# Graph layers: GpSimd also writes one spare column with each row gather

## The reference

```python
s_u = x @ W_u.T + b_u
s_v = x @ W_v.T
e = s_u[src] + s_v[dst]
e = jnp.where(e >= 0, e, 0.2 * e)
m = jax.ops.segment_max(e, dst, num_segments=n_nodes)
e_exp = jnp.exp(e - m[dst])
denom = jax.ops.segment_sum(e_exp, dst, num_segments=n_nodes)
probs = e_exp / denom[dst]
xh = x.reshape(n_nodes, head_dim, num_heads)
msg = xh[src] * probs[:, None, :]
out = jax.ops.segment_sum(msg, dst, num_segments=n_nodes)
```

## Time and profile before

| what | value |
|---|---|
| three timed runs | 5178.16, 5181.27, 5187.05 us (median 5181.27) |
| the profiled execution | span 5191.0 us; the page gives no other time for it |
| busy, share of the span | PE 64%, PEld 46%, DVE 46%, ACT 24%, POOL 44% |
| row gathers on GpSimd | 1856, together 1756.2 us |
| first graph layer | from 509.70 to about 2180 us |
| second graph layer | from 2609.5 to about 4177 us |

### The profile page before, as it was taken

The page is one execution under the profiler, slowest core; times in us unless marked ns, Lnnn a source line. Parts: engine busy times, 40 slices in busy tenths (PEclk is TensorE's granted clock), DMA queues, the critical chain, the costliest instruction groups (busy, mean ns, idle before and its releaser), DMA issues. The chain is left out here.

```text
span 5191.0 us, 77476 instructions
## 1 busy us (share of the span) xinstructions
PE 3340.9 (64%) x13712; PEld 2365.6 (46%) x13713; DVE 2395.9 (46%) x5335; ACT 1269.3 (24%) x5289; POOL 2284.2 (44%) x2343
## 2 busy tenths in 40 slices
PE   4600666667677677698945445545555547999998
PEld 3400333344444444365823333333333335989897
DVE  4500566666666666686434444444444436111111
ACT  2200233333333333342300000000000034333333
POOL 5160455555555555400355555555555540333333
PEclk9855788888888888898967777777777757999999
DMA  8441233323333333200133333333333342666665
GB/s 200 131 126 30 75 76 77 79 76 79 79 78 80 81 81 81 71 0 2 53 77 84 83 82 85 82 82 87 84 84 85 86 125 95 172 170 171 171 171 135
DMA packets 298775, 489.06 MB, mean 94 GB/s; under 512 B 151906, under 2 KB 199984, under 8 KB 298216
## 3 DMA queue, kind: packets, MB, share of 16 engines
q0 software_dynamic: 127312, 325.41, 25.5%
q1 hardware_dynamic: 159535, 159.18, 10.5%
q10 hardware_dynamic: 11872, 3.84, 0.3%
HBM read 430.09 MB, written 58.63 MB: 94 GB/s over the span
## 5 line engine op out<-in xcount | busy, mean ns | idle before, releaser
L865 POOL DMA_INDIRECT g_rows<-rows,g_recs x1856 | 1756.2, 946 | 1624.1 <-DVE g_msg L1019 905.9
L903 PE MATMUL g_pA<-g_msg,k_ident 128*128 128x264 f32 x3712 | 1091.1, 445 | 154.1 <-DVE g_msg L1019 96.1
L903 PEld LDWEIGHTS g_pA<-g_msg,k_ident 128*128 128x128 f32 x3712 | 787.4, 223 | 498.2 <-issue 360.1
L905 PE MATMUL g_pA<-g_accs,k_ident 128*128 128x264 f32 x928 | 368.7, 485 | 840.8 <-DVE g_accs L1026 565.9
L894 PE MATMUL g_pE<-g_ew,g_recT 128*128 128x512 f32 x936 | 581.6, 754 | 296.9 <-ACT g_recT L934 170.8
L1019 DVE TENSOR_TENSOR g_msg<-g_rows,g_pp 128x1024 f32 (+1 forms) x464 | 564.9, 1217 | 293.5 <-ACT g_pp L959 233.8
L905 PEld LDWEIGHTS g_pA<-g_accs,k_ident 128*128 128x128 f32 x928 | 186.5, 224 | 952.3 <-DVE g_accs L1026 624.2
L954 ACT ACTIVATE g_msg<-g_dd (+1 forms) x464 | 113.5, 245 | 1788.0 <-DVE g_dd L1065 1194.5
L894 PEld LDWEIGHTS g_pE<-g_ew,g_recT 128*128 128x128 f32 x936 | 198.9, 230 | 531.2 <-issue 466.1
L1965 PE MATMUL e_pY<-e_w,e_hT 128*128 x1632 | 375.0, 383 | 23.3 <-issue 22.6
L1954 PEld LDWEIGHTS e_pH<-e_xT,e_w 128*128 128x128 f32 x3264 | 382.3, 193 | 5.2
(11 more groups left out here) (410 smaller groups left out, 3580.7 us busy)
## 6 DMA issues: line engine op xcount, KB each, us to landing
e_w<-in_L_ffn_W SPq DMA_DIRECT2D x110, 1024.0 KB
g_rows<-rows,g_recs POOLq DMA_INDIRECT x1856
g_recs<-slots SPq DMA_DIRECT2D x468, 8.0 KB
tok<-e_xall SPq DMA_DIRECT2D x7, 910.0 KB
rows<-p_row SPq DMA_DIRECT2D x50, 119.0 KB
own<-p_row SPq DMA_DIRECT2D x50, 119.0 KB
p_x<-in_x SPq DMA_DIRECT2D x1, 5600.0 KB
own<-p_x SPq DMA_DIRECT2D x1, 5600.0 KB
```

What stands on the lines that cost most here:

```text
L865: pool.indirect_dma_start(out=rows[:, r, j, :], out_offset=None, in_=rows_d, in_offset=bass.IndirectOffsetOnAxis(ap=recs[:, r, 4 * j:4 * j ...
L903: t_.matmul(pA[:, b, 0:MW], K["ident"][:], msg[:, b, j, :], start=(j == 0), stop=False)
L905: t_.matmul(pA[:, b, 0:MW], K["ident"][:], accs[:], start=False, stop=True).then_inc(agg_ok, 1)
```

## The change

A new tile `beat` holds one number per partition. Behind every row gather of both graph layers GpSimd now writes a zero into it, with a memset that raises the new counter `beaten`. Behind each gather but the first of a layer, and ahead of its memset, GpSimd waits until the memset before has raised `beaten`, and raises `pace`. Nobody else reads `beat` or `beaten`.

```diff
@@ -771,6 +771,7 @@
         den = m.sb(L + "den", [Q, H])
+        beat = m.sb(L + "beat", [Q, 1])
         if not vscale:
...
@@ -865,6 +866,10 @@
                             pool.indirect_dma_start(out=rows[:, r, j, :], out_offset=None, in_=rows_d,
                                                     in_offset=bass.IndirectOffsetOnAxis(ap=recs[:, r, 4 * j:4 * j + 1].bitcast(I32), axis=0)
                                                     ).then_inc(rows_in[r], 16)
+                            if not (first and r == 0 and j == 0):
+                                pool.wait_ge(beaten, 4 * C * u + C * r + j)
+                                pool.sem_inc(pace, 1)
+                            pool.memset(beat[:], 0.0).then_inc(beaten, 1)
                 gather(0, True)
                 with pool.Fori(1, n2 + 2) as u:
                     gather(u, False)
```

More of the change, by code:

```diff
@@ L793, in graph @@
         recT_ps = S("recT_ps"); recT_ok = S("recT_ok"); enc_ok = S("enc_ok"); enc_free = S("enc_free"); lane_ok = S("lane_ok")
-        dd_ok = S("dd_ok"); pp_ok = S("pp_ok"); cs_ok = S("cs_ok"); msg_ok = S("msg_ok"); acc_ok = S("acc_ok"); agg_ok = S("agg_ok"); x_ok = S("x_ok")
+        dd_ok = S("dd_ok"); pp_ok = S("pp_ok"); beaten = S("beaten"); cs_ok = S("cs_ok"); msg_ok = S("msg_ok"); acc_ok = S("acc_ok"); agg_ok = S("agg_ok"); x_ok = S("x_ok")
         row_of = lambda ap: ap.rearrange("p a h -> p (a h)")
```

## The result

The changed kernel takes 5212.8 us (median of four runs, 5206.98 to 5218.3), the kernel before 5184.16 us beside it: a ratio of 1.0059, 95% interval 1.0044 to 1.0073. The forecast was 4870 us. The profiled execution's span is 5204.9 us.

A forecast was written before the change was run, and what follows sets the result against it. Bound: a mutual one in both layers, where held engines free no buffers, GpSimd stops, and the overhang drains. GpSimd's 223 us hidden, the wait 0, 315 given back: 5191 - 315 = 4876, said as 4870 us; range 4700 to 5080.

The forecast's parts named there:

- The overhang: Behind each gather something takes 1.43 us while gathers come each 1.25, so 0.18 us piles up per gather in a burst.
- the holds: Stretches in both graph layers when SyncE, VectorE and ScalarE were said to be held until what piles up behind gathers drains.
- The pitch: Time from one gather's start to the next on GpSimd: from 1.25 to 1.37 us, with ends of 1.21 and 1.51.
- The term of 223 us: GpSimd's added time over all gathers, 1856 x 0.12 us, taken to lie under its 905.9 us of standing.
- the relief of 315 us: Half of ScalarE's 284.7 and VectorE's 346.2 us of waits without a named releaser, to be given back in the graph layers.
- hidden: Rival: GpSimd's added work fits into its 905.9 us of standing and the holds stay; time stays at 5181 us; chance 0.14.
- The wait: GpSimd's wait for the memset of one gather earlier, covered by a gather of 0.95 us, so counted as 0.
- Serial: Rival: GpSimd's wait isn't covered, each gather takes 2.00 us, layers 1856 us each, time 5654 us; chance 0.09.
- Stretched holds: Rival: others are held while GpSimd's queue is busy, bursts grow 0.12 us per gather, 5404 us; chance 0.22 with the port.
- The port: Related price: memsets lock the port VectorE and GpSimd share, 0.09 us each, up to +167 us; in stretched holds' 0.22.
- Full relief by self-throttling: Rival: held-back memset completions slow GpSimd to 1.45 us per gather, nothing piles up, layers 1346 us each, 4634 us; chance 0.17.

The follow-up runs named there:

- steps3: Kernel before plus three already fulfilled waits, each with a raise of `pace`, behind each gather in both layers, no memset: 5092.6 us, ratio 0.9850.
- before_again: The kernel before, unchanged, run and profiled once more: 5172.6 us, with 5174.7 beside it.
- l0_steps: Kernel before plus one already fulfilled wait with a raise of `pace` behind each gather, first layer only, no memset: 5137.4 us, ratio 1.0068.

## Why the prediction was wrong

**The overhang: right.** "1.43 us behind each gather, a new one each 1.25" is what the runs bear out from both sides: at 1.25 the holds are there, at 1.44 they are fewer (most of all in the first layer), at 1.52 to 1.54 gone in the second layer and few in the first, and the engines return 1.43 us per gather after the change too. The Trainium skill (Perfetto Trace Analysis, "DMA Instruction — SWDGE (GPSIMD)") says that the profile ends such an instruction when its descriptors are written, and that the DMA engines go on moving data behind that end. The trace agrees: by the DMA packets in the first layer of before, where the recorded gather is 0.95 us long, the first packet of rows starts 1.64 us after the gather's start and the last signal of their landing comes at 2.46 (medians). But these transfers are not what piles up: the twelfth gather of a burst has the same 1.64 and 2.48 us as the first (1.63 and 2.44), so the rows keep up with a gather each 1.25 us while the queue steps fall behind. What it is that holds the other queues, no run showed.

**The pitch: wrong, and this is the step that failed.** The prediction put x, the time from a gather's end to its memset, at 0.16 us from a row of another instruction, and the pitch at 1.37. Measured: x is 0, the memset 0.11, and 0.19 follow; the sum is 1.25. The term of 223 us is 0, and with it goes the relief of 315 us that was to follow from the wider pitch. The low end of the range for x was there (1.21), and the text even said what it means: the memset falls into the gap. But a gap of 0.30 behind every gather, with nothing waiting for anything, is the first place that a small instruction of the same engine goes to; it should have been the value taken. With an unchanged pitch the same sum says no relief, 5181 us. That is the time of the rival "hidden", given 0.14, though it had another reason (holds that the pitch doesn't touch); and the loss of 29 us is outside its 10 us, so no branch of the prediction has the result for its own reason.

**The relief per microsecond: too good as well.** At 1.37 us the text let most holds vanish, 315 us. No run has an even pitch of 1.37. But at 1.44, above the 1.42, only 177 us came back (0.9654), and it took 1.52 to give 330 (0.9363). The spacing has to leave room.

**The wait: half right.** It costs no pitch. What the text didn't see is that it puts two queue steps per gather on GpSimd, which can be held like anyone's. "GpSimd's own waits never took over 17 ns" was read as if GpSimd were exempt; in before its queue had few steps, three to four per chunk.

**The rivals.** Serial (2.00 us per gather): no. Stretched holds: no, the bursts are not longer per gather and the return still follows their number. The port: VectorE's busy time is 2395.9 us before and 2397.0 after, 1.1 us more where this rival had up to 167, so the memsets held it for next to nothing; the rule of the Trainium skill that the prediction cited (SBUF — State Buffer, "SBUF: two separate sides") allows that for a memset, which reads nothing. Full relief by self-throttling: not in the change; steps3 shows something of it (1.36 and 1.43 us inside a chunk, 0.985 of the time), and the time that the text gave it (4634 us) left out that a layer at 1.45 us keeps holds. The busy time of the engines, before and after:

```profile
PE 3340.9 (64%) x13712; PEld 2365.6 (46%) x13713; DVE 2395.9 (46%) x5335; ACT 1269.3 (24%) x5289; POOL 2284.2 (44%) x2343
PE 3379.6 (65%) x13712; PEld 2391.1 (46%) x13713; DVE 2397.0 (46%) x5335; ACT 1267.7 (24%) x5289; POOL 2493.8 (48%) x4199
```

**The 0.6%.** Shown: it is the first layer's (0.79%, against -0.32% in the second), and in that layer a queue step and a memset behind each gather each cost something of their own (0.68 and 0.38%). Argued, not shown: that the loss comes through the holds. For it: the step costs nothing in the version with next to none, and the held time moved the way of the layers (457 to 528 us in the first, 453 to 412 in the second). Against it: held time is a rough measure, since the second layer has 379 to 481 us of it in every version whose gathers follow each other at under 1.5 us without pauses, while its length goes from 1415 to 1567. Open: by which way an added step or memset lengthens the holds of the others, while the pitch and the 1.43 us stay, and why the parts don't add in both layers. The layers' lengths have to do with how the chunks fall into bursts (in before's first layer a chunk takes 7.2 us in bursts of eight gathers and 7.5 in bursts of twelve, medians), but the number of such bursts doesn't decide: with bursts ended by a pause of over 2.0 us from start to start, before has 26 of twelve, before_again 30 and after 37; with 2.4 us it is 39, 41 and 39.

## What to carry to other kernels

Where an engine stands in a short gap behind each of many equal instructions, price a small added instruction at nothing first, and look for what it does to the queue and not to the engine. Where waits without a named releaser end a fixed time per gather after a burst began, space the gathers out until that time is covered with room to spare: here 1.52 us for 1.42, which took 5.5 to 6.4% off the kernel's time. An engine that is not the bound can be too fast.

## What the runs showed of the hardware that was not expected

- Steps of the held queues end together: where two engines' slow steps end within 1.5 us of each other, they end at the same time or 0.70 or 1.40 us apart, GpSimd's among them. Two such steps make about the 1.42 us of a gather.
- The overhang differed from chip to chip (one profile on each of the first three), and the time of before with it. From a burst's first gather to the end of its last slow step, by its number of gathers (bursts of seven and more, first layer, unchanged code): median 1.418, 1.424 and 1.429 us where before takes 5174.7, 5184.2 and 5204.5 us. In l0_steps and l0_perturn, whose first layer is changed and where before takes 5110.4 us, it is 1.41.
- The rows of a burst of gathers land on time while other engines' queues are held: 2.44 us after the start of the first gather, 2.48 after that of the twelfth (medians, first layer of before).
- Memsets in a row overlap: one of 128x88 takes 188 ns, three 0.41 us.
